# One core, conv scans and mixture of experts: norms moved between VectorE and ScalarE, the first conv block in halves, orders written out

## The reference

```python
def conv(x, in_w, in_b, out_w, out_b, gamma, beta):      # H, W, B, D = 16, 16, 8, 64
    inp, og, fg = jnp.split(x @ in_w + in_b, 3, axis=-1)
    inp, og, lam = silu(inp), sigmoid(og), sigmoid(fg)
    inp_o = einsum('...hd,...he->...hde', 1.0 - lam, inp)        # pairs of channels, E = 2
    s_h, s_w = bidir_scan(inp_o, lam) along H, along W           # h_t = lam_t h_{t-1} + inp_t, both ways
    out = einsum('...hde,...hd->...he', s_h + s_w, og)
    out = (out - mean) * rsqrt(var + 1e-5) * gamma + beta
    return out @ out_w + out_b

x = x + conv(ln(x, 1e-6)); t = tokens(x)
t = t + sum_e gate_e(ln(t)) * ((silu(ln(t) @ w1[e]) * (ln(t) @ w2[e])) @ w3[e])     # 16 experts, hidden 128, top 2
x = x + conv(ln(x, 1e-6)); t = tokens(x)
t = t + sum_e gate_e(ln(t)) * (gelu(ln(t) @ W1[e] + b1[e]) @ W2[e] + b2[e])         # 8 experts, hidden 256, top 2
```

## Time and profile before

| | |
|---|---|
| three runs | 271.37, 274.17, 275.12 us (median 274.17) |
| the profiled execution | 270.85 us |
| its span, first to last instruction | 268.9 us |
| busy: TensorE, VectorE | 221.9 us (83%), 211.9 us (79%) |
| busy: ScalarE, GpSimd | 159.5 us (59%), 117.7 us (44%) |
| mean granted TensorE clock | 0.962 of full speed |

### The profile page before, as it was taken

How to read it: one execution, slowest core, us unless ns; L and a number is a source line. 1 busy time by engine, 2 the same in 40 slices (tenths; PEclk the granted TensorE clock), 3 DMA queues, 4 the chain that set the end, 5 groups by cost and what they waited for, 6 DMA issues and landing times. The chain is left out here.

```text
span 268.9 us, 3812 instructions
## 1 busy us (share of the span) xinstructions
PE 221.9 (83%) x966; PEld 127.5 (47%) x966; DVE 211.9 (79%) x607; ACT 159.5 (59%) x298; POOL 117.7 (44%) x179
## 2 busy tenths in 40 slices
PE   0844268976988987899997999598599989999993
PEld 0633157634635554555562653165275454465541
DVE  5498989986999799999799999989975886342135
ACT  2552937464833665238695299129978975947550
POOL 5051992263816431267442646357335307413111
PEclk9999959999999999799998899989989999999999
DMA  1399307193049100490009500000700420410701
GB/s 35 85 197 194 75 0 157 44 211 66 0 94 201 24 1 2 109 203 6 1 7 210 102 0 1 0 4 4 156 4 0 110 49 4 123 36 22 158 20 39
DMA packets 18545, 18.52 MB, mean 69 GB/s; under 512 B 5350, under 2 KB 12284, under 8 KB 18524
## 3 DMA queue, kind: packets, MB, share of 16 engines
q1 hardware_dynamic: 18524, 18.28, 32.7%
...
## 5 line engine op out<-in xcount | busy, mean ns | idle before, releaser
L1209 PE MATMUL SPARE<-tok_z,up_hi 128*128 128x512 f32 x192 | 86.0, 448 | 4.6 <-DVE hidden L1114 2.9
L1210 PE MATMUL SPARE<-tok_z,up_lo 128*128 128x512 f32 x192 | 78.4, 408 | 0.0
L553 POOL TENSOR_TENSOR total<-total,weighted 128x512 f32<-128x512 f32 x39 | 50.3, 1290 | 59.0 <-DVE weighted L1135 36.5
L1322 PE MATMUL SPARE<-hidden,down 128*64 128x512 f32 x256 | 67.3, 628 | 1.5 <-DVE hidden L1114 0.9
L832 ACT ACTIVATE silu_h<-SPARE 128x512 f32<-128x512 f32 x64 | 37.1, 593 | 42.4 <-PE SPARE L1210 37.5
L1209 PEld LDWEIGHTS SPARE<-tok_z,up_hi 128*128 128x128 f32 x192 | 37.7, 197 | 51.1 <-issue 24.4
L1114 DVE TENSOR_TENSOR hidden<-silu_h,SPARE 128x512 f32<-128x512 f32 x64 | 42.5, 677 | 6.0 <-PE SPARE L1322 2.9
L1210 PEld LDWEIGHTS SPARE<-tok_z,up_lo 128*128 128x128 f32 x192 | 37.9, 197 | 5.4
L838 ACT ACTIVATE hidden<-SPARE,expert_bias 128x512 f32<-128x512 f32 x32 | 21.8, 681 | 14.4 <-PE SPARE L1210 12.6
L1322 PEld LDWEIGHTS SPARE<-hidden,down 128*64 128x64 f32 x256 | 14.4, 137 | 27.1 <-issue 17.9
L845 ACT ACTIVATE hidden<-SPARE,expert_bias 128x512 f32<-128x512 f32 x32 | 21.8, 680 | 2.1 <-PE SPARE L1210 2.1
...
## 6 DMA issues: line engine op xcount, KB each, us to landing
gates_b<-gates_dram SPq DMA_DIRECT2D x6, 1024.0 KB, 10.0
...
```

What stands on the lines that cost most here:

```text
L553: nc_engine.tensor_tensor(t, t, weighted[:, q % WEIGHED_RING, :], ALU.add).then_inc(s_sum, 1)
L1209: nc.tensor.matmul(dst, hi, z, start=True, stop=False)
L1210: return nc.tensor.matmul(dst, lo, z, start=False, stop=True)
L1322: last = nc.tensor.matmul(spare("down", q)[k * D:(k + 1) * D, :], w, hidden[:, at, :], start=(j == 0), stop=(j == chunks - 1))
```

## The change

- `NORM_BY_SCALAR` becomes `{"a": (2, 3, 4), "e": (2, 3, 4)}`, in numbers of chunks. A chunk is a part of a unit: unit 0 is cut into chunks 0 and 1 of one image each, and unit u from 1 on is chunk u + 1. So ScalarE normalises units 1, 2 and 3 in both norms, and VectorE all others. Where ScalarE normalises, the low part is now GpSimd's (`low_parts`), not VectorE's.
- All conv stages and both norms of unit 0 run twice on half as many columns.
- `b_res` is one `scalar_tensor_tensor` for each tile in place of two instructions for all; `top` and `pick` are one stage without the cast of the indices; the gate weights are split into high and low parts by a new stage `gate_w` on VectorE, and the logits are fp32r products of twice as many columns whose halves VectorE adds.
- In the first layer `down` works two pairs in one go (`DOWN_GROUP`).
- `sum_h` writes to PSUM and `sum_w` to SBUF, where before it was the other way.
- The scheduler is gone; the order of each engine and the users of each bank are written out (`ORDER`, `BANK_USES`). The loads on SyncE are issued as before.

```diff
-NORM_BY_SCALAR = {"a": (3, 4, 5, 6, 7), "e": (2, 3, 4, 5, 6, 7)}
+CHUNKS = ((0, 0, 1), (0, 1, 1)) + tuple((u, 0, GB) for u in range(1, UNITS))
+
+NORM_BY_SCALAR = {"a": (2, 3, 4), "e": (2, 3, 4)}
-DOWN_BANKS = 2
+DOWN_GROUP = (2, 1)
...
+ORDER = {
...
+    "DVE": (
+        "gate_w0 a_stats0 a_stats1 in_w0 a_parts0 b_wide0 a_parts1 b_cols0 v_wide0 v_cols0 a_stats2 add_w0 out_w0 "
...
+            def low_parts(n, c):
+                k, t = c % 2, slice(0, chunk_tiles(c))
+                pool.wait_ge(s_high[n], by_scalar_up_to(n, c))
+                if c >= 2:
+                    pool.wait_ge(s_turn[n], c - 1)
+                nc.gpsimd.tensor_tensor(parts[n][:, k, t, 1, :], norm[n][:, k, t, :], parts[n][:, k, t, 0, :],
+                                        ALU.subtract).then_inc(s_low[n], 1)
...
+            def gate_weights():
+
+                high, low = gate_parts[:, :, 0, :], gate_parts[:, :, 1, :]
+                for l in range(LAYERS):
+                    dve.wait_ge(s_small[l], 16 * 3)
+                    e = EXPERTS[l]
+                    last = nc.vector.tensor_copy(high[:, l, 0:e], gate_raw[:, l, 0:e])
+                link(last)
+                for l in range(LAYERS):
+                    e = EXPERTS[l]
+                    last = nc.vector.tensor_tensor(low[:, l, 0:e], gate_raw[:, l, 0:e], high[:, l, 0:e].bitcast(fp32),
+                                                   ALU.subtract)
+                last.then_inc(s_gate_w, 1)
...
-                link(nc.vector.tensor_tensor(conv_y[:, :, :], heads_of(u)[1],
-                                             rstd["b"][:, u % 2, :].unsqueeze(2).broadcast_to([P, TILES, D]), ALU.mult))
-                dve.wait_ge(s_biased, u + 1)
-                r = group_rows(u)
-                nc.vector.tensor_tensor(r, r, by_tile(conv_y[:, :, :]), ALU.add).then_inc(s_conv, 1)
+                dve.wait_ge(s_biased, c + 1)
+                r, y = chunk_rows(c), heads_of(c)[1]
+                for t in range(chunk_tiles(c)):
+                    part = r[:, t // HALF, t % HALF, :]
+                    last = nc.vector.scalar_tensor_tensor(part, y[:, t, :], rstd["b"][:, c % 2, t:t + 1], part,
+                                                          ALU.mult, ALU.add)
+                last.then_inc(s_conv, 1)
...
-                    z = tok_z[:, u % 2, t * P:(t + 1) * P].bitcast(fp32)
-                    last = nc.tensor.matmul(spare("logits", u)[:, t * e:(t + 1) * e], z, gate_raw[:, l, 0:e],
-                                            start=True, stop=True)
+                    last = nc.tensor.matmul(
+                        spare("logits", u)[:, t * 2 * e:(t + 1) * 2 * e].rearrange("p (k e) -> p k e", k=2),
+                        tok_z[:, u % 2, t * P:(t + 1) * P], gate_parts[:, l, :, 0:e], start=True, stop=True)
...
+            def down(first):
+                u = PAIR_UNIT[first]
+                l = layer(u)
+                for q in range(first, first + DOWN_GROUP[l]):
+                    wait_bank(pe, "down", q)
+                    wait_hidden(pe, 2 * q + 1)
```

More of the change, by code:

```diff
@@ L81, in chunk @@
     return next(c for c, (layer_, first, end) in enumerate(UP_CHUNKS) if layer_ == l and first <= e < end)
-LENGTH = {
-    "a_stats": 1.35, "a_rstd": 1.6, "a_norm": 1.8, "a_parts": 1.3, "a_turn": 0.5, "a_z": 0.55,
-    "p_f": 0.5, "p_i": 0.5, "p_o": 0.5, "t_f": 0.6, "t_i": 0.6, "t_o": 0.6, "lam_fw": 0.55, "lam_rw": 0.55, "lam_fh": 1.0, "lam_rh": 1.0, "value": 0.65,
-    "add_w": 0.63, "add_h": 1.0, "fwd_w": 1.13, "rev_w": 1.13, "fwd_h": 1.13, "rev_h": 1.13,
-    "sum_w": 0.63, "sum_h": 0.63, "sum_wh": 1.0, "gate_o": 0.65,
-    "heads": 1.05, "b_stats": 0.95, "b_rstd": 1.6, "b_bias": 0.7, "b_res": 1.0,
-    "e_stats": 1.35, "e_rstd": 1.6, "e_norm": 1.8, "e_parts": 1.3, "e_turn": 0.5, "e_z": 0.55, "logits": 0.95,
-    "top": 0.9, "pick": 1.2, "t_m": 0.2, "gates": 1.5, "g_turn": 0.5, "g_copy": 0.55, "g_send": 2.2, "g_back": 9.5,
-    "x_turn": 0.5, "x_res": 1.0, "up_a": 0.48, "up_b": 0.48, "act": 0.5, "act_b": 0.6, "hid": 0.62, "down": 1.2, "weigh": 0.65, "add": 1.3,
-    "in_w": 1.8, "b_wide": 0.7, "b_turn": 0.4, "b_cols": 0.3, "v_wide": 0.3, "v_turn": 0.3, "v_cols": 0.3,
-    "out_w": 0.8, "products": 3.0, "biases": 0.7, "round": 0.6, "split": 1.4}
@@ new lines, in stages_of, with drained_by @@
+def stages_of(names):
+    return [(name.rstrip("0123456789"), int(name[len(name.rstrip("0123456789")):])) for name in names.split()]
+def drained_by(kind, i):
+    if kind == "up_b":
+        return ("act_b" if step_layer(i) else "hid", i)
+    return (DRAINED_BY[kind], i)
+def schedule():
+    bank_of, bank_after = {}, {}
+    for bank, names in enumerate(BANK_USES):
+        reader = None
+        for stage in stages_of(names):
+            bank_of[stage], bank_after[stage] = bank, reader
+            reader = drained_by(*stage)
+    return {engine: stages_of(names) for engine, names in ORDER.items()}, bank_of, bank_after
@@ L634, in _ @@
                 broadcast_gates(u)
[L635 removed]
+                if u >= 2 and layer(u - 2):
                     store_rows(u - 2)
```

762 lines of the change are left out of this document (315 added, 447 removed), and 89 rows, old and new, of tables (BANK_USES, ORDER).

## The result

The changed kernel takes **257.12 us** (median of four runs, 256.76 to 257.32); the kernel before takes 272.77 us on the same chip (four runs, 269.29 to 275.12). The ratio is 0.951, with a 95% interval from 0.9445 to 0.9575. The forecast was 266 us with a range from 256 to 277. The profiled execution took 257.32 us, its span is 255.4 us; the sum had made 262.9 us for it. Medians are over all executions of a run; three of these, of 741 us (`norms_scalar`), 704 us (`down_single`) and 513 us (`start_best`), stand far from the others of their kernels and move the medians by under 0.6 us, and the ratios leave slow executions out.

The account below looks back on a forecast made before the run. VectorE's queue was taken to set the pace until unit 6's gate, TensorE after: 195.48 + 6.65 − 6.5 = 195.6, plus 65.3 gives 260.9, with 1.95 around it 262.9; forecast median 266 us, range 256 to 277.

Parts of the forecast that it names:

- rival 2: VectorE's stops in the middle go altogether, and most of the fill's too: 259 us; chance 0.15.
- G: When VectorE reaches the output gate of unit 6: 195.48 us before, 195.6 forecast, 193 to 199 as the sign.
- The factor 1.012: Scaling from profiled time to median, since the three runs' median was 1.2% above the profiled one: 262.9 to 266 us.
- The start, +7.6 us: Head of VectorE's queue: `gate_w0` waits for gate weights until 10.60 us, where work began at 3.00; nothing hides it.
- VectorE's work to G, −0.95 without the start: VectorE's terms up to G: 0.55, −0.6, −2.4, +1.3, −1.1 and +1.3, making +6.65 with the start's 7.6.
- The residual, −2.4: `b_res` on VectorE: 24 instructions at 0.17 us, 4.1 us, instead of 6.5 us for six units before G.
- Norms, −0.6: VectorE up to G: 15.5 us before; after, unit 0's halves about 4.9 and five full norms at 2.0, 10.0.
- rival 3: Contention with GpSimd: five full norms before G take 3.5 us each instead of 2.0, +7.5 us, 274 us; chance 0.11.
- Top two, 0, and one moved across G, +1.75: VectorE: a cast of 0.17 us goes, an add of about 0.2 comes; `top5`, thirteen small instructions, moves before G.
- Stops, −6.5: VectorE's waits in the middle, 9.7 us: two thirds go; bounds 0 and 9.7.
- Grouped downs: TensorE before G: 16 fewer changes of kind save 4.8 us, hidden while VectorE is the pace.
- Rival 4: Late TensorE: first up product at 55.7 us, 188 us of work after it, stops stay 30.4 us: 279 us; chance 0.12.

Follow-up runs that it names:

- norms_scalar: Changed kernel with the eight norms of the second layer given back to ScalarE, their low parts to GpSimd: 282.07 us.
- down_single: Changed kernel with the first layer's down products one pair at a time, the even pair three up stages ahead of the odd one: 269.53 us.
- start_best: Changed kernel with the gate weights behind out_w, both behind v_cols, and the halves' row inputs ahead of units 1 and 2's statistics: 251.30 us, ratio to before 0.928.
- before_norms: Kernel before with only the norms assigned as in the change, all orders set anew by its planner: 277.56 us, ratio 1.020.
- whole: Changed kernel with unit 0's conv block in one piece instead of two halves: 257.11 us.
- before_parts: Kernel before with the new assignment of norms, the one-instruction residual and the new sums, orders by its planner: 273.37 us, ratio 1.0038.

## Why the prediction was right, and where it was off

The direction, the place of the gain and the shape were right; 266 was 8.9 us too high. The measured time is 1 us inside the lower end of the range and below even rival 2's 259, so there is luck in the range having held. G at 189.85 is before the 193 to 199 that was named as a sign, and 5.75 us before the sum's 195.6: 4.75 of them are VectorE's work and 1.0 its stops. Step by step:

- **The factor 1.012.** 3.1 us of the error. It carried the scatter of the kernel before (269.3 to 275.1) over to a kernel whose runs agree within 0.6 us. On the profiled execution's own scale the error is 262.9 against 257.3.
- **The start, +7.6 us.** VectorE's first statistics come at 10.97 us, and the stops of the fill within 0.6 us of the walk. "Nothing hides it" was too strong: moving `gate_w` gave back 4.1 us, and 2.8 stood before the rows of units 1 to 3.
- **VectorE's work to G, −0.95 without the start: the step that failed in size.** It is −5.7. The largest piece is an edit that was put at nothing without a reason: the sums, −2.3 us by the account above, 3.5 us of time when undone. The list of the change names that edit, and the prediction has no term for it; the row of `sum_wh` with its 1.02 us beside 0.68 for the other sums was there to be asked about.
- **The residual, −2.4.** From start to start one was 0.2 us and not 0.17, and the rows give −2.1 (6.8 to 4.7); undoing it cost 3.7. Undisturbed the two forms cost the same, so the saving is what the old form loses beside GpSimd. The mean of 0.66 us for its add held that, without my saying so.
- **Norms, −0.6.** Rows give +0.1, with two errors against each other. By their durations the five full ones took 1.6 us each and not 2.0; one subtraction of 0.67 us was all that was held up. So **rival 3** did not happen: the held-up casts of full norms, 1.26 and 1.25 us, come behind G. And unit 0's halves took 7.7 us and not 4.9, since the e-steps of the halves ran in GpSimd's company (means of 0.77 and 0.90 us, where the same forms of the a-norm take 0.29 and 0.23).
- **Top two, 0, and one moved across G, +1.75.** Together −0.1: six of them take 10.4 us where five took 10.5. The old five held one `pick` of 1.29 us and one `margin` of 0.78 us, where the new ones take 0.23 and 0.17 at the last place before G. That is the second largest miss, 1.9 us; with the sums it makes 4.2 of the 4.75, and the rest are small terms of both signs.
- **`in_w1`, −1.1.** As forecast: 4.2 to 3.1.
- **Halving.** Right that it earns nothing: 257.11 without it.
- **Stops, −6.5.** −7.5 in idle time. Between the forecast and **rival 2**: of the middle's 12.1 us 7.1 went, of the fill's 5.7 us 0.4. The longest wait left in the middle is for ScalarE, 1.4 us in all (line 1022), which the prediction had named as a sign of being wrong; it is too small to matter here.
- **Grouped downs "matter before G only", hidden.** Wrong: 2.7 us of 3.6 show. With VectorE at 96% and TensorE at 94% neither hides the other.
- **TensorE from G, 65.3.** 65.55. The logits' groups there are 0.54 and 0.55 us and not 0.4.
- **Rival 4** did not happen: TensorE's stops from the first up product to G add up to 7.9 us (132.76 less 124.86), and to 14.0 up to the end. By the prediction's own figures it would have set the time from 17 us of stops on (the span of 260.9 less 243.7), not 25. Its "as I expect again" failed too: the first up products after ran at full clock, 0.22 to 0.24 us apart, since the clock had risen at 56.2 us.

**What makes the stops go** is the open part of the reason I gave. I said that VectorE has two units' scans in hand. Shown is that it is not the assignment of norms by itself (`before_norms` is slower), nor the halves (`whole`), and that residual and sums added to that assignment leave VectorE 22.6 us idle up to G; grouping gives 2.7 us. Between 273.4 and 257.1 lie 16.3 us, and what those two kernels do not share besides halves and groups is the written-out orders and bank users, GpSimd's low parts, the top two in one stage and the single-pass logits. The orders are what I take for the main cause, by exclusion and because sixteen downs placed early in them cost 10 us (`down_single`). That is an argument: their share alone has not been measured, nor that of the low parts, the top two and the logits.

## What to carry to other kernels

Price a part in the version in which it is to work: the residual gave 2 us at most in the old kernel and 3.7 us in the new one, where VectorE's queue has few stops. And take a bundle of parts apart before calling it worthless: in `before_parts` some 4 us of gain and 5 of loss stood side by side. For each edit that looks neutral (a destination in the other memory, a sum that swaps its operands) look up the row of every instruction that reads the new place. Of two forms with the same undisturbed price take the one that reads one operand from PSUM, when GpSimd is busy beside it.

## What the runs showed of the chip

- **A turned read from SBUF.** The sum whose operand is read with a step of 16 elements takes 1.04 us on the mean for 512 columns with that operand in SBUF and 0.68 with it in PSUM, as much as with no turn (0.59 against 0.42 for 256). The Trainium skill, "SBUF — State Buffer", section "Door 1: The DMA port swizzle (why `[64,N]` ≈ `[32,N]`)", has a note that an access leaving a 16-byte line pays a penalty, four fp32 being the free step; the trace agrees for SBUF. The same note has finer lines for PSUM and speaks of matmuls; on VectorE no penalty shows.
- **TensorE's clock between the first up product and G.** It falls to the lower of its two levels (1.2 of 2.4 GHz) in four stretches before (from 108, 146, 173 and 194 us, the last one past G), and in none after. In the fill it is the other way round: low from 33.5 to 40.4 us before and from 39.2 to 56.2 us after, where TensorE was busy 6.88 of 17 us and VectorE was the pace. The windows of one of the four:

```profile
105.00:108.00 3.00, 1.06 (x6) 0.60 (x6) 2.97 (x5) 0.59 (x1) 0.72 (x2) 1.00 0.02 5
108.00:109.00 1.00, 0.67 (x2) 0.62 (x3) 1.00 (x3) 0.00 (x0) 0.05 (x1) 0.82 0.15 33
109.00:110.00 1.00, 1.00 (x4) 0.71 (x4) 1.00 (x3) 0.60 (x1) 1.00 (x1) 0.50 0.00 0
110.00:111.00 1.00, 1.00 (x5) 0.35 (x4) 1.00 (x3) 0.00 (x0) 0.23 (x1) 0.50 0.00 0
111.00:112.00 1.00, 1.00 (x5) 0.24 (x4) 0.97 (x2) 0.60 (x1) 0.00 (x0) 0.50 0.60 223
```

TensorE had been busy 1.06 of the 3 us ahead of it. During the stretch it reads as fully busy, at half the speed: busy share alone hides such a loss. In `norms_scalar` a stop of 1.85 us for a silu was followed by the same (0.50 from 104 to 107 us). The windows of one microsecond in these four stretches fall short of full clock by 1.7 us each, at most 6.8 us of TensorE's time; how much of it reached the end before, where VectorE was the pace, was not measured.
